# A weight quantisation is moved from inside phase 3 to the head of phase 4 of a two-layer kernel

## The chip, the cores and the metric

The kernel runs on all 8 cores of one Trainium2 chip, as one program on each core, with no exchange between the cores. The metric is the device time of one execution in microseconds (us), that of the slowest core.

## The reference, cut to what matters

Two transformer-like layers run in sequence on activations of 2 x 8192 tokens and 1024 features. What counts here is the last feed-forward block. Both of its weights are quantised to three levels before they are used:

```python
def weight_quant(w):
    scale = 1.0 / jnp.clip(jnp.mean(jnp.abs(w)), 1e-05)
    return jnp.clip(jnp.round(w * scale), -1, 1) / scale

def bit_linear(x, w):
    xq = x + jax.lax.stop_gradient(act_quant(x) - x)
    wq = w + jax.lax.stop_gradient(weight_quant(w) - w)
    return jnp.einsum('bsd,hd->bsh', xq, wq)

# L1_ffn: w1 is 4096 x 1024, w2 is 1024 x 4096, both float32
h = bit_linear(x, w1)
h = silu(depthwise_conv1d(h) )
y = bit_linear(h, w2)
# whole model, in order; each block is followed by x = layernorm(x + block(x))
# L0 attention, L0 feed-forward (quantised, low-rank), L1 attention, L1 feed-forward
```

The mean of the absolute values is taken over a whole weight, so a weight has to be read once for the mean and a second time to be rounded.

## The kernel before

Each core has its own share of the tokens as columns (`NCOL` = 2080, features on the partitions in `DCH` = 8 chunks of 128), and the program has four phases, one for each block of the model, with a wait of all engines between them (`_phase_gate`). The instruction stream of each engine is in the order in which the Python code emits it: nothing is reordered, so an instruction that waits holds up everything behind it on its engine. SP issues most DMAs, and its queue is in order too.

**Phase 3** (`emit_phase3`, layer 1 attention) first normalises, then runs two halves over the `WvT` weight and two over `WuT`. Each half loads 1024 weight columns into `w3w` by a DMA from GpSimd's queue and runs over `NT` = 5 tiles of `ST` = 416 columns: that is 20 tiles. In each tile `emit_xn` makes the normalised input (one small matmul, one ScalarE copy `a3sb`, eight GpSimd products `XB<-X,a3sb`), and then 8 output chunks of 8 matmuls each go to `p3psv`, ScalarE applies Silu into `p3u`, and VectorE writes `g_all`. After the 20 tiles GpSimd issues the load of `w3o` (`WoT`), 640 matmuls `p3psv<-g_all,w3o` follow, and a post-layernorm ends the phase.

**The quantisation of w1 and w2** is cut into steps by `wquant_steps` (line 1873) with units of 128 x 512: for each weight an `init`, 64 steps `p1` (load of 256 KB, VectorE sum of absolute values), one step `mid` (mean, its reciprocal, both spread over the partitions), 64 steps `p2` and a `fin`: 131 steps for a weight, 262 in all. A `p2` step is: SP loads the unit again (`wqs`), VectorE multiplies by the scale and adds a large constant (`wqc<-wqs`), GpSimd subtracts the constant (`wqc<-wqc,wqg`), which leaves the rounded value, VectorE clips to -1..1 (`wqc<-wqc`), VectorE multiplies by 1/scale into bfloat16 (`wqo<-wqc`), and SP stores the unit to device memory (`w1qd` or `w2qd`). SP waits for the last VectorE operation of a unit before it issues its store, and only then issues the next unit's load, so the second load buffer isn't used ahead of time in this pass. After each of the 20 tiles `drain_wq(k, 6)` emits six steps, 120 in all; when the tiles are done `drain_wq(k)` emits the other 142 in one piece, and all engines wait for the end of that before the load of `w3o`.

**Phase 4** (`emit_phase4`) starts when `X` has been spilled to device memory. It loads the two quantised weights, 8.4 MB each in bfloat16, and runs eight column blocks. It also has an `if not io.get("wquant_done")` branch (line 1329), which before isn't taken, with two calls of `emit_wquant` (line 1242). That function does the same arithmetic in the same order on the same engines, from SP's queue too, but with units that are a whole chunk: 8 units of 128 x 4096 for w1 (2 MB of float32 each), 32 of 128 x 1024 for w2 (512 KB each). Its second pass is, cut:

```python
for ch in range(nch):
    b = ch % 2
    vd = k.dma(q, wstr[b][:], src_h[:, ch, :], f"wq{q}e{b}")      # SP: load a unit
    v1 = k.tsc("vector", scr[:], wstr[b][:], swpp[:, 0:1], MAGIC, ALU.mult, ALU.add, inc="p4q1")
    k.wait("gpsimd", "p4q1", v1)
    v2 = k.tt("gpsimd", scri, scr[:], mgt[:].broadcast_to([128, width]), ALU.subtract, inc="p4q2")
    k.wait("vector", "p4q2", v2)
    v3 = k.tsc("vector", scri, scri, 1.0, -1.0, ALU.min, ALU.max, inc="p4q3")
    v4 = k.tsc("vector", wqo[b][:], scri, swpp[:, 1:2], None, ALU.mult, inc="p4q4")
    k.wait(q, "p4q4", v4)                                         # SP waits, then stores
    k.dma(q, wq_dram[:, ch * width:(ch + 1) * width], wqo[b][:], f"wq{q}o{b}")
```

Here too the load of the next unit stands behind the store of this one on SP's queue. In the first pass the load of unit `ch` waits for the reduction of unit `ch - 2`, so two loads can be under way.

Of the kernel before, what the change touches and what calls it, by code (L numbers as in the profile page):

```python
# [261 lines left out]
def alloc_common(k, io, stream=True):  # L262
    if stream:
        k.t["X"] = k.sb("X", [128, DCH * NCOL], F32)
        k.t["XB"] = k.sb("XB", [128, DCH * NCOL], BF16)
    k.t["ones1_f"] = k.sb("ones1f", [1, 128], F32)
    k.t["onescol_f"] = k.sb("onescolf", [128, 1], F32)
    k.t["onesn_bf"] = k.sb("onesnb", [128, 1], BF16)
    k.t["iden_f"] = k.sb("idenf", [128, 128], F32)
    k.t["iden_b"] = k.sb("idenb", [128, 128], BF16)  # L270
    k.t["eps_ln"] = k.sb("epsln", [128, 1], F32)
    k.t["neg1"] = k.sb("neg1", [128, 1], F32)
    k.t["ones1_b"] = k.sb("ones1b", [1, 128], BF16)
    k.dma("sync", k.t["ones1_f"][:], io["ones1"], "cst")
    k.dma("gpsimd", k.t["onesn_bf"][:], io["onesn"], "cstg")
    k.dma("gpsimd", k.t["ones1_b"][:], io["ones1"], "cstg")
    k.dma("sync", k.t["iden_f"][:], io["iden"], "cst")
    k.dma("gpsimd", k.t["iden_b"][:], io["iden"], "cstg")
    k.memset("vector", k.t["eps_ln"][:], 1e-5, inc="cstv")
    k.memset("vector", k.t["neg1"][:], -1.0, inc="cstv")  # L280
    k.memset("vector", k.t["onescol_f"][:], 1.0, inc="cstv")
    for eng in ("tensor", "vector", "scalar"):
        k.wait(eng, "cst", k.val("cst"))
        k.wait(eng, "cstg", k.val("cstg"))
        k.wait(eng, "cstv", k.val("cstv"))
# [11 lines left out]
def emit_load_stream(k, io):  # L297
    X, XB = k.t["X"], k.t["XB"]
    src = io["xin"].rearrange("(c p) n -> p c n", p=128)
    k.dma("sync", X[:].rearrange("p (c n) -> p c n", c=DCH), src, "ldx")  # L300
    k.dma("gpsimd", XB[:].rearrange("p (c n) -> p c n", c=DCH), src, "ldxb")
    for eng in ("tensor", "vector", "scalar", "gpsimd"):
        k.wait(eng, "ldx", k.val("ldx"))
        k.wait(eng, "ldxb", k.val("ldxb"))
# [402 lines left out]
def io_names(io):  # L707
    return {kk: ap.tensor.name for kk, ap in io.items() if hasattr(ap, "tensor")}
# [1092 lines left out]
def _phase_gate(k, sem, val):  # L1801
    for eng in K.ENGINES:
        k.wait(eng, sem, val)


def build_fused():
    stack = ExitStack()
    nc = bass.Bass("TRN2", target_bir_lowering=False)
    io = declare_io_fused(nc)
    with stack:  # L1810
        k = K(nc, stack)
        alloc_common(k, io, stream=False)
        k.push_scope()
        k.t["X"] = k.sb("X", [128, DCH * NCOL], F32)
        k.t["XB"] = k.sb("XB", [128, DCH * NCOL], BF16)
        emit_load_stream(k, io)
        s1, v1 = emit_phase1(k, io)
        _phase_gate(k, s1, v1)
        k.release_sems(("p1", "ldx"))
        k.dma("sync", io["xspill"], k.t["X"][:], "fsp1")  # L1820
        k.wait("sync", "fsp1", k.val("fsp1"))
        io["x1ref"] = io["xspill"]
        s2, v2 = emit_phase2(k, io)
        _phase_gate(k, s2, v2)
        k.release_sems(("p2", "dq_", "fsp1"))
        io["wquant_on"] = True
        io["wquant_done"] = True
        s3, v3 = emit_phase3(k, io)
        _phase_gate(k, s3, v3)
        k.release_sems(("p3", "wq_"))  # L1830
        k.dma("sync", io["xspill"], k.t["X"][:], "fsp2")
        k.wait("sync", "fsp2", k.val("fsp2"))
        _phase_gate(k, "fsp2", k.val("fsp2"))
        k.pop_scope()
        io["xstate"] = io["xspill"]
        s4, v4 = emit_phase4(k, io)
        k.wait("sync", s4, v4)
        k.finalize()
    return nc, io_names(io)
# [13 lines left out]


FUSED = True


def kernel_fused(**inputs):
    P = host_prep(inputs)
    Qs = [host_core_inputs(P, c) for c in range(NCORES)]  # L1860
    nc, nm = _built("fused", build_fused)
    maps = [{nm[kk]: v for kk, v in fused_in_map(P, Qs[c]).items()} for c in range(NCORES)]
    r = run_bass_kernel_spmd(nc, maps, core_ids=list(range(NCORES)))
    return host_assemble_yout([r.results[c][nm["yout"]] for c in range(NCORES)])
# [102 lines left out]
```

How the kernel before makes its waits and increments, by code:

```python
    def _post(self, eng, fn, inc, inck):  # L93
        if inc is None:
            self.ops[eng].append(fn)
            return None
        s = self._sem(inc)
        s[1] += inck
        h = s[0]
        self.ops[eng].append(lambda e, fn=fn, h=h, k=inck: fn(e).then_inc(h, k))
        return s[1]
# [1 line left out]
    def wait(self, eng, sem, v):  # L103
        if not v:
            return
        h = self._sem(sem)[0]
        assert v <= self._sem(sem)[1], f"wait beyond emitted incs: {sem} {v}"
        self.ops[eng].append(lambda e, h=h, v=v: e.wait_ge(h, v))
# [50 lines left out]
    def barrier(self, tag):  # L159
        s = self._sem("bar_" + tag)
        h = s[0]
        s[1] += len(self.ENGINES)
        tgt = s[1]
        for eng in self.ENGINES:
            self.ops[eng].append(lambda e, h=h: e.nop().then_inc(h, 1))
        for eng in self.ENGINES:
            self.ops[eng].append(lambda e, h=h, t=tgt: e.wait_ge(h, t))
```

## Time and profile before

| | us |
|---|---|
| median of 2 runs | 6435.69 |
| the 2 runs | 6421.44, 6449.95 |
| profiled execution | 6414.45 |
| its slowest core (core 2), first to last instruction | 6412.9 |
| the other cores | 6379.2 to 6409.1 |

Busy shares of the span on core 2: TensorE 35%, VectorE 31%, GpSimd 23%, ScalarE 13%; the DMA queues moved 258.92 MB. No engine is near full, so the time is a chain of waits between engines, and what a stage costs has to be read in that stage. The granted TensorE clock is given as a share of 2.4 GHz; 0.50 is its lower level, 1.2 GHz. Names in the rows are the program's buffers; "L136" is the line of the helper that records the operation. A unit of KB in a DMA row is 1024 bytes.

### The profile page before, as it was taken

Reading aid. Unit: us, or ns where it says so; the run is one execution under the profiler, and the core shown is the slowest. Engines: PE = TensorE matmul, PEld = TensorE weight load, DVE = VectorE, ACT = ScalarE, POOL = GpSimd, SP = SyncE. Lnnn points to the kernel's source line nnn. Section 1 sums busy time; section 2 is a strip of 40 time slices with the busy share of each in tenths; the row PEclk is TensorE's granted clock in tenths of the full one; section 3 lists DMA queues with packets and bytes.
Section 4 is the critical chain, followed back from the end, with each engine's and each line's share of the span. In section 5 each row is a group of like instructions: output and inputs, shape, how many; then the busy total and the mean of one; then the engine's idle time right before and its main releaser. Section 6 shows DMA issues by size and latency. Waiting matters only on the chain.

```text
span 6412.9 us, 40031 instructions; the slowest of 8 cores (6379.2 to 6412.9 us)
## 1 busy us (share of the span) xinstructions
PE 2256.0 (35%) x11801; PEld 1181.2 (18%) x11808; DVE 1972.1 (31%) x3257; ACT 856.2 (13%) x1551; POOL 1444.9 (23%) x1032
## 2 busy tenths in 40 slices
PE   1345423634636633532120000722424334323243
PEld 0111101211212211211010000411313223222132
DVE  0023432333333343432222222233333243333333
ACT  0000032322322223110000000020000000010000
POOL 0000030111101133322220111333243333332333
PEclk8665556766767765766565555855656556665566
DMA  9830033011030011221213221131000000000000
GB/s 150 112 46 1 0 85 85 1 54 52 1 92 7 1 54 25 73 59 40 53 39 103 73 59 55 27 112 53 14 0 14 14 0 14 1 13 14 0 14 7
DMA packets 167364, 258.92 MB, mean 40 GB/s; under 512 B 20681, under 2 KB 99666, under 8 KB 165330
## 3 DMA queue, kind: packets, MB, share of 16 engines
q1 hardware_dynamic: 116818, 202.25, 10.2%
q0 software_dynamic: 50336, 54.11, 6.2%
q8 instruction: 102, 1.67, 0.1%
q14 instruction: 108, 0.88, 0.1%
HBM read 268.22 MB, written 42.21 MB: 48 GB/s over the span
## 4 chain that ended last, share of the span: by engine, by line
PE 33%; DMA 19%; DVE 19%; POOL 14%; issue 8%; ACT 5%; SPq 1%; DVEq 1%; another core or an unknown queue 0%; POOLq 0%; ACTq 0%
PE p4pm L120 8%; PE psm L120 7%; PE p3psv L120 6%; DMA wqsw2T<-w2T 5%; POOL p4tB L136 5%; POOL p4tA L136 4%; DMA xkv<-xT 4%; POOL XB L136 3%; DMA wqsw1T<-w1T 3%; DVE p4tA L136 2%; DMA qbuf<-qTw 2%; DVE Y L136 2%; DVE X L136 2%; DVE p4cmt L148 2%; DMA p4x<-xspill 2%
## 5 line engine op out<-in xcount | busy, mean ns | idle before, releaser
L120 PE MATMUL p3psv<-XB,w3w 128*128 128x416 bf16 x1280 | 273.0, 382 | 432.9 <-POOL XB L136 432.7
L136 POOL TENSOR_TENSOR Y<-Y,p2asb 128x416 f32<-128x416 f32 x120 | 144.4, 1236 | 1211.3 <-ACT p2bsb L127 1211.3
L120 PE MATMUL p4pm<-p4xq,w1q 128*128 128x260 bf16 x2048 | 266.2, 297 | 399.2 <-DVE p4h L136 316.5
L136 POOL TENSOR_TENSOR p4tB<-p4h,cw 128x2048 f32<-128x2048 bf16 x64 | 296.9, 4640 | 414.1 <-DVE p4h L136 281.9
L120 PE MATMUL p4pm<-p4c,w2q 128*128 128x256 bf16 x2048 | 241.9, 284 | 229.9 <-DVE p4c L140 229.9
L120 PEld LDWEIGHTS p4pm<-p4xq,w1q 128*128 128x128 bf16 x2048 | 211.6, 105 | 457.5 <-issue 407.4
L120 PE MATMUL p3psv<-g_all,w3o 128*128 128x416 bf16 x640 | 115.4, 344 | 468.2 <-DMA w3o<-WoT 468.2
L120 PEld LDWEIGHTS p4pm<-p4c,w2q 128*128 128x128 bf16 x2048 | 207.8, 102 | 267.5 <-issue 235.5
L120 PEld LDWEIGHTS p3psv<-XB,w3w 128*128 128x128 bf16 x1280 | 136.6, 108 | 567.0 <-issue 490.7
L120 PE MATMUL psm<-VB,w2b 128*128 128x416 bf16 x960 | 213.9, 371 | 14.5 <-ACT t1s L127 14.5
L136 DVE TENSOR_TENSOR p4tA<-p4tA,p4tB 128x2048 f32<-128x2048 f32 x64 | 146.7, 2293 | 234.5 <-POOL p4tB L136 234.4
L136 POOL TENSOR_TENSOR XB<-X,a3sb 128x416 bf16<-128x416 f32 x160 | 167.2, 1077 | 219.1 <-ACT a3sb L127 219.1
L123 PE MATMUL p4pt<-idenb,p4c 128*128 128x128 bf16 x512 | 64.7, 306 | 417.0 <-ACT p4c L132 333.9
L120 PE MATMUL psm<-XB,w2b 128*128 128x416 bf16 x960 | 194.9, 347 | 14.2 <-ACT t1s L127 14.2
L136 POOL TENSOR_TENSOR p4tA<-p4c,p4rb 128x2048 f32<-128x2048 bf16 x32 | 130.5, 4077 | 300.7 <-ACT p4rb L127 232.9
L136 POOL TENSOR_TENSOR X<-X,asb_pl 128x416 f32<-128x416 f32 x120 | 154.7, 1321 | 187.4 <-ACT bsb_pl L127 187.4
L127 ACT CAST XB<-X 128x416 bf16<-128x416 f32 x162 | 82.8, 537 | 819.7 <-POOL X L136 645.1
L120 PE MATMUL pskv<-xkv,qkvT 128*128 128x512 bf16 x249 | 99.3, 565 | 246.4 <-DMA xkv<-xT 245.5
L136 POOL TENSOR_TENSOR wqcw2T<-wqcw2T,wqgw2T 128x512 f32<-128x512 f32 x64 | 66.5, 1038 | 497.6 <-DVE wqcw2T L140 497.6
L136 DVE TENSOR_TENSOR X<-X,bsb_pl 128x416 f32<-128x416 f32 x120 | 151.5, 1329 | 84.2 <-POOL X L136 84.1
L136 DVE TENSOR_TENSOR p4h<-p4pm,p4rb 128x260 bf16<-128x260 f32 x256 | 109.1, 429 | 189.8 <-PE p4pm L120 158.7
L136 POOL TENSOR_TENSOR wqcw1T<-wqcw1T,wqgw1T 128x512 f32<-128x512 f32 x64 | 66.5, 1038 | 444.9 <-DVE wqcw1T L140 444.9
(243 smaller groups left out, 4369.0 us busy)
## 6 DMA issues: line engine op xcount, KB each, us to landing
xkv<-xT POOLq DMA_DIRECT2D x32, 1024.0 KB, 16.1
wqsw1T<-w1T SPq DMA_DIRECT2D x128, 256.0 KB, 2.9
wqsw2T<-w2T SPq DMA_DIRECT2D x128, 256.0 KB, 3.0
qbuf<-qTw SPq DMA_DIRECT2D x96, 256.0 KB, 3.6
sbuf<-sTe SPq DMA_DIRECT2D x96, 256.0 KB, 4.1
xspill<-X SPq DMA_DIRECT2D x2, 8320.0 KB, 25.9
X<-xin SPq DMA_DIRECT2D x1, 8320.0 KB, 48.0
xrb<-xspill SPq DMA_DIRECT2D x5, 1664.0 KB, 9.2
```

What stands on the lines that cost most here:

```text
L120: e.matmul(o, l, r, start=s, stop=p), inc, 1)
L123: return self._post("tensor", lambda e, o=out, i=in_, d=iden: e.transpose(o, i, d), inc, 1)
L127: return self._post(eng, lambda e, o=out, i=in_: e.copy(o, i), inc, 1)
L136: e.tensor_tensor(o, a, b, p), inc, 1)
L148: e.tensor_reduce(o, i, AXX, p, apply_absolute_value=a), inc, 1)
```

## The change

Phase 3 is built with `wquant_on` unset, and phase 4 with `wquant_done` unset.

```diff
@@ build_fused
         k.release_sems(("p2", "dq_", "fsp1"))
-        io["wquant_on"] = True
-        io["wquant_done"] = True
+        if WQ_IN_P3:
+            io["wquant_on"] = True
+            io["wquant_done"] = True
         s3, v3 = emit_phase3(k, io)
@@
 FUSED = True
+WQ_IN_P3 = False
```

So `wquant_steps` is never called, the `drain_wq` calls in phase 3 find no steps and emit nothing, and the fence after phase 3's statistics is for GpSimd alone. In phase 4 the two calls of `emit_wquant` are now emitted, ahead of the loads of the quantised weights: w1 with 8 units of 4096 columns, then w2 with 32 units of 1024 columns.

## Rows read from the trace of the kernel before

**Rows 1.** The page, the span in 40 slices of 160 us: TensorE's busy tenths.
```profile
PE   1345423634636633532120000722424334323243
```

**Rows 2.** Chain that ended last, 2400 to 4500 us: start us, us, what.
```profile
2524.37 8.18 POOL XB L136 x8
2547.86 8.33 POOL XB L136 x8
...
2659.93 8.18 POOL XB L136 x8
...
2780.07 17.88 DMA w3w<-WuT
2799.56 8.18 POOL XB L136 x8
...
2950.41 8.56 POOL XB L136 x8
...
3008.17 8.55 POOL XB L136 x8
...
4007.06 25.55 DMA w3o<-WoT
```

**Rows 3.** Instructions on w1's load buffer: duration min/median/max ns, first to last start.
```profile
L140 DVE TENSOR_SCALAR wqcw1T<-wqsw1T,wqww1T x64: 479/486/489, 2858.6 to 3437.4; 128x512 f32<-128x512 f32 x64
```

**Rows 4.** The same of w2's load buffer, scratch and output buffer.
```profile
L148 DVE TENSOR_REDUCE wqpw2T<-wqsw2T x64: 678/686/687, 3445.6 to 3561.0; 128x1 f32<-128x512 f32 x64
L140 DVE TENSOR_SCALAR wqcw2T<-wqsw2T,wqww2T x64: 486/486/489, 3568.2 to 4001.5; 128x512 f32<-128x512 f32 x64
...
L136 POOL TENSOR_TENSOR wqcw2T<-wqcw2T,wqgw2T x64: 1038/1038/1040, 3568.8 to 4002.2; 128x512 f32<-128x512 f32 x64
L140 DVE TENSOR_SCALAR wqcw2T<-wqcw2T x64: 426/427/428, 3570.0 to 4003.3; 128x512 f32<-128x512 f32 x64
L140 DVE TENSOR_SCALAR wqow2T<-wqcw2T,wqww2T x64: 485/486/489, 3570.5 to 4003.9; 128x512 bf16<-128x512 f32 x64
```

**Rows 5.** Timeline 3552 to 3580 us, w2's first rounding step: start us, us, instruction.
```profile
3568.19 0.49 DVE L140 TENSOR_SCALAR wqcw2T<-wqsw2T,wqww2T 128x512 f32<-128x512 f32 x1 [4.49 <-DMA wqsw2T<-w2T]
...
3571.08 0.33 SPq L116 DMA_DIRECT2D w2qd<-wqow2T  x1
3571.45 0.43 SPq L116 DMA_DIRECT2D wqsw2T<-w2T  x1
3575.14 0.49 DVE L140 TENSOR_SCALAR wqcw2T<-wqsw2T,wqww2T 128x512 f32<-128x512 f32 x1 [4.14 <-DMA wqsw2T<-w2T]
```

**Rows 6.** Granted clock by stretch: from:to, us, PE busy, PEclk, DMA share, GB/s.
```profile
4008.00:4034.00 26.00, 0.94 (x3) 0.50 0.91 162
4034.00:4045.00 11.00, 11.00 (x51) 0.79 0.00 0
```

**Rows 7.** Groups with shapes, phase 4 (4360 us on): busy, mean ns of one, idle before.
```profile
L136 POOL TENSOR_TENSOR p4tA<-p4c,p4rb 128x2048 f32<-128x2048 bf16 x32 | 130.5, 4077 | 300.7 <-ACT p4rb L127 232.9 <-DVE p4c L140 67.8
L136 POOL TENSOR_TENSOR p4tA<-p4tA,cb 128x2048 f32<-128x2048 f32 x32 | 115.2, 3601 | 81.3 <-DVE p4tA L136 81.3
L148 DVE TENSOR_REDUCE p4cmt<-p4pt 128x1 f32<-128x1024 bf16 x78 | 95.6, 1225 | 142.2 <-PE p4pt L123 142.2
L140 DVE TENSOR_SCALAR p4tA<-p4tA 128x2048 f32<-128x2048 f32 x32 | 39.3, 1227 | 180.9 <-POOL p4tA L136 180.9
```

**Rows 8.** DMA issues of the whole span: count, KB each, median us from issue to landing.
```profile
wqsw1T<-w1T SPq DMA_DIRECT2D x128, 256.0 KB, 2.9
wqsw2T<-w2T SPq DMA_DIRECT2D x128, 256.0 KB, 3.0
...
xspill<-X SPq DMA_DIRECT2D x2, 8320.0 KB, 25.9
...
xrb<-xspill SPq DMA_DIRECT2D x5, 1664.0 KB, 9.2
p4x<-xspill SPq DMA_DIRECT2D x8, 1040.0 KB, 8.3
w1qd<-wqow1T SPq DMA_DIRECT2D x64, 128.0 KB, 1.7
...
w2q<-w2qd SPq DMA_DIRECT2D x1, 49.4
```

## The prediction

> **What bounds the kernel now.** I read the page's slices first. TensorE is nearly empty from slice 22 to 25 and thin from 18 on [rows 1]; that is the stretch of phase 3 in which the quantisation runs. The chain that ended last then tells what fills it. In the first half of phase 3 a tile begins with eight GpSimd products and the next begins 23.5 us later (2524.37 to 2547.86), and a half of five tiles with its weight load takes 135.6 us (2524.37 to 2659.93) and 139.6 us (2659.93 to 2799.56) [rows 2]. In those halves the six steps behind each tile are of kind `p1`, and the first tile, with none before it, is as long as the others, so `p1` costs nothing there: its loads and sums lie beside the next tile's GpSimd products and matmuls. From the mean on it is another picture: the tile of 2950.41 is followed by that of 3008.17, 57.8 us later [rows 2]. Six `p2` steps stand in VectorE's, GpSimd's and SP's order between two tiles, and TensorE's next tile needs GpSimd's products. They hide almost nothing: 57.8 - 23.5 = 34.3 us for six steps, 5.7 each, against 6.9 where they run alone ((4001.5 - 3568.2) / 63) [rows 4]. The last 10 `p2` steps of w1 and all of w2 then run with no tile beside them: w1's last begins at 3437.4 [rows 3], and the load of `w3o` is issued at 4007.06 [rows 2]. So about 570 us of the path is the bare drain, and some 380 more are the steps put between tiles. A step itself is latency: a load of 256 KB that lands after 3.0 us [rows 8], and four operations that wait for each other.
>
> **The change, part by part.**
>
> *Removed from phase 3.* Without steps the 20 tiles should run like the first two halves. The mean of a half with its load is (135.6 + 139.6) / 2 = 137.6 us; the load's share is 2799.56 - 2780.07 = 19.5 us. From 2524.37 the four halves end after 3 x 137.6 + (137.6 - 19) = 531 us, at 3056 us. There GpSimd issues the load of `w3o`, which now is at 4007.1 [rows 2]. The gain is 951 us. The u halves have one VectorE operation for each output chunk where the v halves have two, so nothing there makes them longer. Bounds for the tile: 23.5 to 24 us, that is 5 us either way on the sum.
>
> *Not changed.* The matmuls on `w3o` begin with a clock of 0.50 after a wait for that load and rise in the first 11 us [rows 6]; after the change they come after the same 26 us wait. Phase 4's blocks begin after a stretch without matmuls in both kernels. I count nothing for the clock. The fences that fall away in phase 3 cost nothing, since the tile behind them waits for the weight load anyway. The spill of `X` and the loads of the quantised weights are as before.
>
> *Added at the head of phase 4.* Nothing runs beside it, so each microsecond counts. I need the operations at 4096 and 1024 columns, which the trace doesn't have, and scale each from two widths.
>
> - VectorE scaling and clipping: 427 ns at 512 columns [rows 4] and 1227 at 2048 [rows 7], so 0.521 ns a column more: 0.69 us at 1024, 2.29 at 4096. The two with a scale from memory are 0.06 longer (486) [rows 4]: 0.75 and 2.35. Bounds: in proportion from 486 at 512 (3.9 at 4096), and twice the 2048 row (2.45).
> - GpSimd's subtraction: 1038 ns at 512 with a broadcast second input [rows 4], 3601 at 2048 with a broadcast one, 4077 with one full row of 256 repeated [rows 7]. The operand here is a broadcast, so I go by 3601: 1.67 ns a column, 1.89 us at 1024 and 7.02 at 4096. Upper bound: eight times 1038, 8.3 us. No row gives a lower price.
> - VectorE's sum: 686 ns at 512 [rows 4], 1225 at 1024 [rows 7]: 1.05 a column, 4.45 us at 4096.
> - Loads: 256 KB land after 2.9 to 3.0 us. The big contiguous transfers are the spill, 8320 KB in 25.9 us (329 GB/s with its start), and the two quantised weights, 16.8 MB in 49.4 us (340 GB/s), with all eight cores about at the same place [rows 8]. At 340 GB/s each further MB takes 2.9 us: 3.7 us for 512 KB, 2.9 + 1.84 MB / 340 GB/s = 8.3 for 2 MB. Bounds: the 1664 KB load at 185 GB/s and the 1040 KB load at 128 GB/s [rows 8], both with short rows (1664 and 1040 bytes), where these have 16 and 4 KB; so I go by 340.
>
> First pass of w1: eight loads, two under way, in effect a stream of 16.8 MB, 49 us at 340 GB/s, and 2 us of start and the last sum of 4.5: 56. First pass of w2: at 512 columns one unit takes (3561.0 - 3445.6) / 63 = 1.83 us, which is (load 2.98 + sum 0.69) / 2 [rows 4]. At 1024 it is (3.75 + 1.23) / 2 = 2.5, 32 units 80, with the start 83.
>
> Second pass. A step of 512 columns has period 3575.14 - 3568.19 = 6.95 us: 2.80 from the first VectorE operation to the end of the last (2.44 of work, 0.36 between), 0.46 until the next load is issued behind the store, and 3.69 until that has landed [rows 5]. For w2: 0.75 + 1.89 + 0.69 + 0.75 + 0.36 = 4.45; 0.46; and 3.69 + 0.77 for the larger load + 0.38 for the larger store ahead of it = 4.84. Period 9.75, times 32 = 312 us. For w1: 2.35 + 7.02 + 2.29 + 2.35 + 0.36 = 14.4; 0.46; and 3.69 + 5.4 for 1.84 MB more of load + 2.7 for 0.92 MB more of store = 11.8. Period 26.6, seven of them and a first of 8.5 + 14.4: 209 us.
>
> The two means: the last sum ends at 3561.0 + 0.7 [rows 4] and the first rounding operation begins at 3568.2 [rows 5], 6.5 us, of which 3.0 are the first load, counted already: 3.5 each, 7 for two. The last stores have to land: 128 KB take 1.7 us [rows 8], so 1.7 + 2.7 = 4.4 for w1's 1 MB, and 1.7 + 0.4 for w2's, with the issue 2.7.
>
> Gates and memsets I put at 1.5 (estimated from the 0.46 between waits). Sum: 56 + 209 + 83 + 312 + 7 + 4.4 + 2.7 + 1.5 = 676 us. Fewer and larger units help: 64 rounding steps of 6.9 us are 440 in w2 and 32 of 9.75 are 312; for w1 eight of 26.6 are 209.
>
> *Two prices from the Trainium skill, by themselves.* Its page GPSIMD Engine Reference, section Performance versus the Vector engine, gives 4497 ns for a two-input GpSimd operation at 2048 float32 columns; the trace has 3601 and 4077 for a broadcast second input, which is lower, so I go by the trace. By the page the subtraction would be an estimated 9.0 us at 4096 and 2.3 at 1024, and the sum 676 + 8 x 2.0 + 32 x 0.4 = about 705 us. Its page DMA: Bandwidth & Descriptors, section Anatomy of one DMA, fits 2.0 us plus the bytes at 436 GB/s for one transfer, an estimated 6.8 us for 2 MB where I have 8.3, and by it the sum would be some 45 us smaller, first passes included; the trace has 340 GB/s for its longest transfers, so I keep that.
>
> **Net.** -951 + 676 = -275 us. The sum is made on the profiled execution: 6414 - 275 = 6139 us. The median of the two runs is 21 us above that execution, and 6436 - 275 = 6161. I forecast between the two: 6150 us, 4.4% less than the median.
>
> **The rivals.**
>
> - *Loads are slow at this size when eight cores read at once.* The added work moves 67.1 MB of loads and 16.8 of stores, 83.9 MB, of which I priced nearly all at 340 GB/s, 247 us. For it: 2 MB units make the DMA engines busier than anything in phase 3 now. Against it: the 49.4 us of the two weights. At the 185 GB/s of the 1664 KB load it is 454 us, 207 more: 6150 + 207 = 6357 us, 1.2% less than before, so no change that can be told.
> - *The same with the rate of the 1040 KB load, 128 GB/s:* 655 us, 408 more, 6558 us, slower by 1.9%. It has eaten the gain of 286 us from 157 GB/s down (83.9 MB / 533 us), and slower by over 2% begins at 127. Only short rows have shown such a rate.
> - *The interleaved steps were in fact covered,* and the long tiles are long for another reason (GpSimd's products wait for something else). Then phase 3 gives back only the bare drain, 4007 - 3437 = 570 us, and the time is 6150 + 381 = 6531 us, 1.5% slower. What speaks for it is that something must overlap; the Trainium skill's page Trainium Kernel Development and Optimization, section Best Practices, asks for double-buffering so that DMA and compute overlap, and moving the work to a stage of its own gives that up. Against it: 57.8 us a tile with six rounding steps, 23.5 with six sums or none [rows 2], and the next load stands behind the store on SP's queue, so there is no overlap within a step now either. By the page's rule the trace disagrees for `p2` and agrees for `p1`.
> - *Transfers start sooner than I have it.* The 128 KB stores land in 1.7 us, which is 1.3 besides the bytes where I have 2.1 for a load: 0.8 less on 40 rounding loads and half of it on 40 in the first passes, 48 us less, 6102. It is a variant of the forecast, in its range.
>
> **How the numbers follow.** The forecast with that variant has 0.90, loads at the middle rate 0.05, at the low rate 0.02, covered steps 0.03. A measurement of this kernel tells about 2% (129 us) from no change. Faster by over 2% is below 6307 us: all of the first case but little, 0.91. Within 2%: most of the rest, 0.07. Slower by over 2%: 0.02. For the range I take the bounds of the unknown prices: below, the variant at 6102, less 11 for the lower base, 5 for the tiles and 26 for what else may be cheaper: 6060. Above, GpSimd in proportion (16 more in all), VectorE in proportion (8 x 4.2 and 32 x 0.6, 53) and all bytes at 300 GB/s, a quarter of the way to 185 (33): 102 more, 6250. About 0.85 of the chance is in it.
>
> **What would show each step.** Tiles of phase 3 all 23 to 24 us apart, and `w3o` issued near 3056. In phase 4: eight GpSimd subtractions of about 7.0 us, 32 of 1.9; load landings near 11 and 4 us (8 and 4 in the first pass); a w2 rounding period near 9.75 and a w1 one near 26.6; 676 us from the end of the spill to the load of `w1q`. The forecast is wrong if the tiles stay long without steps, if the landing of 2 MB is over 15 us, or if phase 4's blocks take another time than now.

## The result, and the profile after

| | before | after |
|---|---|---|
| median of all runs, us | 6448.3 (10 runs) | 6102.2 (11 runs) |
| ratio, with its 95% interval | | 0.9468 (0.9436 to 0.9500) |
| profiled execution, us | 6414.5 | 6166.7 |

The forecast was 6150 us with a range of 6060 to 6250. In a second comparison on another occasion the ratio was 0.9521 (0.9476 to 0.9565), so the gain is 308 to 343 us, where the sum had 275.

The page of the changed kernel, its slices (154 us each), again shows four empty slices of TensorE, but one phase later: they lie between phase 3's layernorm and phase 4's blocks. What is gone are the thin slices ahead of them, 18 to 21 in [rows 1].

```profile
PE   1345431663662663355575000012432424324243
DMA  9840015003003001000010534240000000000000
```

In the profiled execution, 65 us above the median, cores 0 to 3 show a granted clock of 0.62 and spans about 40 us longer than cores 4 to 7 at 0.635, so phase 3 is read on core 5 (the chain that ended last: start us, us, what), the head of phase 4 on core 1, the slowest.

```profile
2526.26 8.18 POOL XB L136 x8
2550.25 8.32 POOL XB L136 x8
...
2795.68 8.18 POOL XB L136 x8
2819.78 8.19 POOL XB L136 x8
...
3001.16 8.49 POOL XB L136 x8
3025.08 8.19 POOL XB L136 x8
3049.72 27.16 DMA w3o<-WoT
```

The tiles are 23 to 24 us apart in the last half as in the first, where they were 57.8 [rows 2], and the load of `w3o` is issued 523 us after the first tile. Then the head of phase 4, the first units of w1 and the last of w2:

```profile
3406.22 24.31 DMA xspill<-X
3431.03 15.03 DMA wqsw1T<-w1T
...
3496.50 7.74 DMA wqsw1T<-w1T
3504.33 2.36 DVE wqcw1T L140
3506.83 7.02 POOL wqiw1T L136
3513.95 2.31 DVE wqiw1T L140
3516.35 2.37 DVE wqow1T L140
3519.15 9.19 DMA wqsw1T<-w1T
3528.51 2.36 DVE wqcw1T L140
...
4059.95 2.03 DMA w2qd<-wqow2T
4065.28 49.70 DMA p4x<-xspill
```

A w1 unit takes 24.2 us (3504.33 to 3528.51), of which 9.2 are the landing of its load; the first load, with no store ahead of it, lands after 7.7. The same for w2 on core 1, from the instructions on its load and scratch buffers and a piece of the timeline:

```profile
L148 DVE TENSOR_REDUCE wqpw2T<-wqsw2T x32: 1219/1220/1221, 3697.2 to 3773.8; 128x1 f32<-128x1024 f32 x32
L140 DVE TENSOR_SCALAR wqcw2T<-wqsw2T,wqww2T x32: 753/753/755, 3781.7 to 4055.3; 128x1024 f32<-128x1024 f32 x32
L136 POOL TENSOR_TENSOR wqiw2T<-wqcw2T,wqgw2T x32: 1892/1892/1892, 3782.6 to 4056.3; 128x1024 f32<-128x1024 f32 x32
```

```profile
3794.99 0.33 SPq L116 DMA_DIRECT2D w2qd<-wqow2T  x1
3795.40 0.38 SPq L116 DMA_DIRECT2D wqsw2T<-w2T  x1
3799.12 0.75 DVE L140 TENSOR_SCALAR wqcw2T<-wqsw2T,wqww2T 128x1024 f32<-128x1024 f32 x1 [4.21 <-DMA wqsw2T<-w2T]
3800.08 1.89 POOL L136 TENSOR_TENSOR wqiw2T<-wqcw2T,wqgw2T 128x1024 f32<-128x1024 f32 x1 [6.82 <-DVE wqcw2T L140]
3802.08 0.69 DVE L140 TENSOR_SCALAR wqiw2T<-wqiw2T 128x1024 f32<-128x1024 f32 x1 [2.20 <-POOL wqiw2T L136]
3802.95 0.75 DVE L140 TENSOR_SCALAR wqow2T<-wqiw2T,wqww2T 128x1024 bf16<-128x1024 f32 x1 [0.18 <-DVE wqiw2T L140]
```

The period is (4055.3 - 3781.7) / 31 = 8.83 us. The load was issued right behind the store at 3795.40 and used at 3799.12, 3.7 us later. The step of [rows 5] had 3.69 us for 256 KB, but on core 2. On core 1 of both kernels these loads land after 2.9 us (256 KB) and 3.5 us (512 KB) at the median, so the larger load does take longer.

All kernels side by side, in stages that the same four instructions bound on each core: the first tile of phase 3, the issue of `w3o`'s load, the issue of the spill behind phase 3, the issue of `w1q`'s load. Each number is the median over the eight cores of one profiled execution, in us. The lines "before" and "changed" are of the first comparison, "changed, again" to "sums in phase 3" of a second, "before, again" and the last three of a third.

| kernel | to the first tile | tiles and steps | `w3o`, layernorm | spill and head of phase 4 | rest |
|---|---|---|---|---|---|
| before | 2521 | 1463 | 267 | 25 | 2114 |
| before, again | 2546 | 1470 | 267 | 25 | 2115 |
| changed | 2561 | 531 | 280 | 660 | 2104 |
| changed, again | 2532 | 530 | 266 | 663 | 2104 |
| steps after the tiles | 2525 | 1601 | 269 | 25 | 2113 |
| w1 in units of 1024 | 2534 | 521 | 269 | 773 | 2111 |
| sums in phase 3 | 2529 | 543 | 267 | 506 | 2109 |
| next load ahead | 2530 | 520 | 266 | 459 | 2105 |
| ... and rounding on VectorE | 2532 | 521 | 268 | 364 | 2108 |
| all three | 2537 | 546 | 268 | 210 | 2111 |

So 936 us leave the stage of the tiles and 637 come in at the head of phase 4.

### The profile page after: what moved, and what is told of

It is laid out like the page before. It is cut to its first block, busy times and chain, and to the rows that moved or that the text cites. A ratio compares the mean times of both kernels' runs of the same rounds, so it can differ in the third digit from the quotient of the medians.

```text
span 6165.1 us, 38230 instructions; the slowest of 8 cores (6101.2 to 6165.1 us)
## 1 busy us (share of the span) xinstructions
PE 2357.5 (38%) x11808; PEld 1200.6 (19%) x11808; DVE 1902.6 (31%) x2905; ACT 857.7 (14%) x1551; POOL 1424.6 (23%) x944
## 4 chain that ended last, share of the span: by engine, by line
PE 36%; DVE 19%; DMA 17%; POOL 15%; issue 7%; ACT 5%; SPq 1%; DVEq 0%; ACTq 0%; POOLq 0%; another core or an unknown queue 0%
PE psm L120 8%; PE p4pm L120 8%; PE p3psv L120 7%; POOL p4tB L136 5%; DMA xkv<-xT 4%; POOL p4tA L136 4%; DMA wqsw2T<-w2T 3%; POOL XB L136 3%; DVE p4tA L136 3%; DMA qbuf<-qTw 2%; DVE Y L136 2%; DMA wqsw1T<-w1T 2%; DVE X L136 2%; DMA p4x<-xspill 2%; DVE p4cmt L148 2%
## 5 line engine op out<-in xcount | busy, mean ns | idle before, releaser
L120 PE MATMUL p3psv<-XB,w3w 128*128 128x416 bf16 x1280 | 308.5, 418 | 191.1 <-POOL XB L136 190.3
L120 PE MATMUL psm<-VB,w2b 128*128 128x416 bf16 x960 | 233.4, 396 | 14.5 <-ACT t1s L127 14.5
L120 PE MATMUL psm<-XB,w2b 128*128 128x416 bf16 x960 | 216.3, 375 | 14.2 <-ACT t1s L127 14.2
L123 PE MATMUL p4pt<-idenb,p4xq 128*128 128x128 bf16 (+1 forms) x192 | 24.3, 305 | 496.6 <-DVE p4xq L128 454.2
L144 DVE SCALAR_TENSOR_TENSOR X<-psm,biasA,X 128x416 f32<-128x416 f32 x120 | 78.1, 651 | 269.6 <-PE psm L120 269.6
L136 DVE TENSOR_TENSOR Y<-Y,p2bsb 128x416 f32<-128x416 f32 x120 | 120.5, 1004 | 126.2 <-POOL Y L136 126.2
L148 DVE TENSOR_REDUCE p4cmt<-p4pt 128x1 f32<-128x1024 bf16 (+1 forms) x88 | 107.7, 1224 | 154.8 <-PE p4pt L123 154.8
```

Source lines behind the costliest of these rows:

```text
L120: e.matmul(o, l, r, start=s, stop=p), inc, 1)
L123: return self._post("tensor", lambda e, o=out, i=in_, d=iden: e.transpose(o, i, d), inc, 1)
L136: e.tensor_tensor(o, a, b, p), inc, 1)
L144: e.scalar_tensor_tensor(o, a, s, b, p0, p1), inc, 1)
L148: e.tensor_reduce(o, i, AXX, p, apply_absolute_value=a), inc, 1)
```

## The experiments

### The steps moved behind the tiles, nothing else

The kernel before with both `drain_wq(k, 6)` calls taken out:

```diff
                       ALU.mult, ALU.add, inc=f"p3mx{oc % 2}")
-            drain_wq(k, 6)
@@
                 k.tt("vector", gch, gch, uch, ALU.mult, inc=f"p3mx{oc % 2}")
-            drain_wq(k, 6)
```

> The kernel before with the two drain calls behind the 20 tiles taken out: all 262 steps of 512 columns run in one piece behind the tiles, nothing else changes. My theory (a rounding step is a chain that covers nothing, a sum step between tiles is free): the tiles are 23.5 to 24 us apart throughout, as in the first halves; the piece takes 2 x (64 x 1.83 + 6.5 + 64 x 6.9 + 2) = about 1135 us where it was 566; the load of w3o comes at 3056 + 1135 = about 4190 us, 185 us later than before, ratio to before about 1.029. Rival (the long tiles had another reason, the steps in them were covered): the tiles of the u halves stay near 58 us, and the time is about 565 us longer, ratio 1.09. Rival (it was the interleaving itself that cost, and the size of a unit doesn't matter): the piece takes no more than the 630 us that the same work takes at the head of phase 4, ratio about 0.95.

Measured: 1.0251 (1.0210 to 1.0291), which is 161 us (135 to 187). The tiles are 22.5 to 24.2 us apart in all four halves; these are some of the last half (chain that ended last), and the roundings of w1 behind them (scratch buffer of w1):

```profile
2940.40 8.18 POOL XB L136 x8
2963.47 8.19 POOL XB L136 x8
```

```profile
L140 DVE TENSOR_SCALAR wqcw1T<-wqsw1T,wqww1T x64: 485/486/489, 3184.1 to 3596.8; 128x512 f32<-128x512 f32 x64
```

The rival that the long tiles had another reason falls. The rival that the size of a unit doesn't matter falls too: the bare piece takes 1080 us (1601 less the 521 of tiles alone) for the work that the changed kernel does in 637. And it says where the gain of the change does not come from: with the same units, taking the steps out from between the tiles is a loss, 1601 - 1466 = 135 us. The interleaving had been worth something. Of the 120 steps between the tiles 64 are sums, which take 64 x 1.83 = 117 us by themselves (an estimate), and 54 are rounding steps, 5.7 us each between tiles and 6.5 alone. From this comes off what the sums cost the weight loads (below); the 135 us were not split further. I had 185 for it; the piece was 1135 in my sum and 1080 on the chip, since a rounding step takes (3596.8 - 3184.1) / 63 = 6.55 us here, not 6.9.

### The changed kernel again

> The changed kernel once more, unaltered. In its profiled execution the cores 0 to 3 showed a lower clock (0.62) and matmul stretches of 15 to 16 us a tile where cores 4 to 7 had 14 to 14.5 us. Theory: that is of the execution, not of the change; this profile has all cores near 0.64 and a phase 3 from the first tile to the load of w3o of about 524 us on the slowest core, as core 5 had. Rival: the denser matmuls of phase 3 lower the clock on the slowest core each time; then that stretch is again about 550 us.

Measured: 0.9521 (0.9476 to 0.9565). All eight cores are at 0.633 to 0.638, and the stage of the tiles takes 518 to 533 us, where it was 552 on cores 0 and 1 of the first profile. Cores 0 and 1 have 518 and 519 us now, so their long stage belongs to that execution. The groups of the two cores of it, core 1 and then core 5, show the price (busy us, mean ns of one matmul | idle before):

```profile
L120 PE MATMUL p3psv<-XB,w3w 128*128 128x416 bf16 x1280 | 308.5, 418 | 191.1 <-POOL XB L136 190.3 <-ACT p3u L132 0.8
```

```profile
L120 PE MATMUL p3psv<-XB,w3w 128*128 128x416 bf16 x1280 | 279.4, 389 | 190.9 <-POOL XB L136 190.9
```

The idle time is the same, the 29 us are in the matmuls. But the rival holds in part. On six cores of the repeat, 2 to 7, some tiles are 25 to 26 us apart as well; from 2500 to 3080 us the granted clock is 0.70 on core 7 and 0.75 on core 1. In the two kernels that have the rounding steps in phase 3, no tile without such steps is more than 24.2 us behind the one before it in its half. Nor is one in the run with the next load ahead, so the spells come and go also with the tiles of the changed kernel; what starts them is open. They are worth about 10 us of the stage: 530 us against the 520 of undisturbed cores.

### w1 in four times as many units

```diff
-        emit_wquant(k, io, "w1T", io["w1qd"], DCH, DH)
+        emit_wquant(k, io, "w1T", io["w1qd"], DCH, DH, upc=4)   # 32 units of 1024 columns
```

> The changed kernel with w1 quantised in 32 units of 1024 columns in place of 8 of 4096, w2 as it is. My theory (the price of a unit is its fixed part, load latency and waits, plus columns): w1's sums take about 80 us in place of 62, its roundings 32 x 8.8 = 282 in place of 8 x 24.3 = 194, together about 106 us more than the changed kernel, ratio to before about 0.963. Rival (bytes and columns set the cost, the size of a unit does not): no difference to the changed kernel, 0.947.

Measured: 0.9719 (0.9678 to 0.9761), 0.0198 above the changed kernel in the same comparison, which is 127 us; the head of phase 4 takes 773 us, 110 more than 663. The sums and roundings of w1 (instructions on its load buffer):

```profile
L148 DVE TENSOR_REDUCE wqpw1T<-wqsw1T x32: 1219/1220/1222, 3392.3 to 3472.9; 128x1 f32<-128x1024 f32 x32
L140 DVE TENSOR_SCALAR wqcw1T<-wqsw1T,wqww1T x32: 752/753/755, 3482.0 to 3760.6; 128x1024 f32<-128x1024 f32 x32
```

82 us of sums and 32 x 8.99 = 288 of roundings, where 80 and 282 were expected. The price of a unit is a fixed part and its columns: a rounding unit took 6.55 us at 512, 8.8 to 9.0 at 1024 and 24.3 at 4096, so about 4.0 us and 5.0 us for each 1024 columns, and only the fixed part can be saved by a larger unit.

### The first pass back in phase 3

The steps keep `p1` and `mid` alone (seven behind each tile), their result `swpp` lives outside the phases, and `emit_wquant` loses its first pass:

```diff
-            drain_wq(k, 6)
+            drain_wq(k, 7)          # both places; steps are 64 sums and the mean, per weight
@@ emit_wquant
-    swpp = k.sb(f"wqw{which}", [128, 2], F32)
-    for ch in range(nch): ...      # loads, sums, mean
+    swpp = k.t["swpp" + which]
```

> The changed kernel with the first pass (sums and means) of both weights put back between the tiles of phase 3 in units of 512 columns, seven steps behind each tile, and only the rounding pass at the head of phase 4. My theory (sum steps between tiles are covered): tiles stay 23.5 to 24 us apart, phase 4's head is shorter by 62 + 82 = 144 us, ratio to before 0.947 - 0.022 = 0.925. Rival (the steps cost in a tile about what they cost alone, 1.8 us each, since VectorE and SP are held): phase 3 is longer by up to 128 x 1.8 = 230 us and the ratio is 0.947 or above.

Measured: 0.9297 (0.9261 to 0.9333), 0.0224 under the changed kernel in the same comparison, 144 us. By stages the head is 157 us shorter and the stage of the tiles 13 longer than in the repeat, 22 longer than in the kernels at 520 or 521. All tiles but the last keep their distance; two other things get longer. One is the weight load between two halves (chain that ended last of this kernel, core 3, then the landings of `w3w`'s loads on core 5 of the changed one, min/median/max us):

```profile
2722.07 8.32 POOL XB L136 x8
...
2745.80 8.32 POOL XB L136 x8
...
2798.13 18.00 DMA w3w<-WuT
...
2937.37 19.14 DMA w3w<-WuT
```

```profile
DMA to landing us min/median/max: 12.9/13.1/13.4
```

The other is the last tile, on the same chain:

```profile
3028.93 8.20 POOL XB L136 x8
...
3053.52 2.60 DMA wqtw2T<-w2T
...
3059.03 0.98 PE wqps L120 x4
3060.01 0.38 PE p3psa L120
...
3061.23 0.24 POOL XB L136
```

So a sum step costs nothing in a tile, but one behind the last tile of a half loads beside the weight that the next half waits for: the three loads inside the stage take 15.3 to 20.7 us over the eight cores, 17.3 at the median, 4 us more each. And the step with w2's mean stands in TensorE's order ahead of the last tile's first matmul and waits for the last sums: that tile comes 32.3 us behind the one before (32.1 to 32.6 on all cores) and not 23.9. Three loads and this one tile make the 22 us.

### The next load ahead of the store

```diff
+    vds = [k.dma(q, wstr[c][:], src_h[:, c, :], f"wq{q}e{c}") for c in range(2)]
     for ch in range(nch):
-        if ch >= 2:
-            k.wait(q, "p4q1", k.val("p4q1") - 1)
-        vd = k.dma(q, wstr[b][:], src_h[:, ch, :], f"wq{q}e{b}")
         ...
+        if ch + 2 < nch:                       # behind the first operation of unit ch
+            k.wait(q, "p4q1", v1)
+            vds.append(k.dma(q, wstr[b][:], src_h[:, ch + 2, :], f"wq{q}e{b}"))
```

> The changed kernel with one order altered in the rounding pass: SP issues the load of unit ch + 2 as soon as unit ch has been read, ahead of the store of unit ch, so the next unit's load no longer stands behind this unit's store. My theory (in a rounding period the load's landing and the arithmetic are added, 9.2 + 14.6 us in w1 and 3.5 + 4.5 in w2): the landing goes out of the chain, periods fall from 24.3 to about 14.5 and from 8.8 to about 4.6 us, in all about 200 us less than the changed kernel, ratio to before about 0.95 - 0.031 = 0.919. Rival (the memory is what limits, with eight cores loading at once): w2's period stays above 6 us and the gain is under 100 us, ratio above 0.935.

Measured: 0.9197 (0.9137 to 0.9257); the head of phase 4 takes 459 us, 204 less (by the two ratios 0.0324, about 208 us). Timeline of two w2 units:

```profile
3644.59 1.89 POOL L136 TENSOR_TENSOR wqiw2T<-wqcw2T,wqgw2T 128x1024 f32<-128x1024 f32 x1 [2.53 <-DVE wqcw2T L140]
...
3649.01 1.89 POOL L136 TENSOR_TENSOR wqiw2T<-wqcw2T,wqgw2T 128x1024 f32<-128x1024 f32 x1 [2.52 <-DVE wqcw2T L140]
```

The period is 4.4 us here and 4.5 over all 32, the arithmetic alone; w1's is 14.4. The landing was in the chain, and the memory keeps up with eight cores at this pace.

### Rounding on VectorE alone

GpSimd's subtraction is folded into the two VectorE operations behind it:

```diff
-        v2 = k.tt("gpsimd", scri, scr[:], mgt[:].broadcast_to([128, width]), ALU.subtract, inc="p4q2")
-        v3 = k.tsc("vector", scri, scri, 1.0, -1.0, ALU.min, ALU.max, inc="p4q3")
-        v4 = k.tsc("vector", wqo[b][:], scri, swpp[:, 1:2], None, ALU.mult, inc="p4q4")
+        v3 = k.tsc("vector", scri, scr[:], MAGIC, 1.0, ALU.subtract, ALU.min, inc="p4q3")
+        v4 = k.tsc("vector", wqo[b][:], scri, -1.0, swpp[:, 1:2], ALU.max, ALU.mult, inc="p4q4")
```

> As the run with the next load ahead, and the four operations of a rounding made three, all on VectorE (scale and add the constant; subtract it and cap at 1; bound at -1 and multiply by 1/scale), so GpSimd and its wait are out of the chain. My theory: a w1 unit takes 3 x 2.35 + 0.2 = 7.3 us if its 2 MB load and 1 MB store keep up (3.1 MB at 340 GB/s are 9.3 us, so rather 9.3), a w2 unit about 2.4 us, another 40 + 70 = 110 us less, ratio about 0.902. Rival (GpSimd's part was already covered by something): within 20 us of the run before it, 0.919.

Measured: 0.9058 (0.9008 to 0.9109), head 364 us, 95 less than the run before it, 110 expected. First operations of a unit on core 4, w1 and w2 (load buffers), two of w1's on the timeline, and the stretch of w1's rounding and that of w2's (from:to, us, ... DVE busy ..., PEclk, DMA share, GB/s):

```profile
L140 DVE TENSOR_SCALAR wqcw1T<-wqsw1T,wqww1T x8: 2347/2353/2354, 3492.8 to 3552.7; 128x4096 f32<-128x4096 f32 x8
```

```profile
L140 DVE TENSOR_SCALAR wqcw2T<-wqsw2T,wqww2T x32: 746/753/755, 3653.6 to 3750.3; 128x1024 f32<-128x1024 f32 x32
```

```profile
3507.06 2.35 DVE L140 TENSOR_SCALAR wqcw1T<-wqsw1T,wqww1T 128x4096 f32<-128x4096 f32 x1
...
3517.13 2.35 DVE L140 TENSOR_SCALAR wqcw1T<-wqsw1T,wqww1T 128x4096 f32<-128x4096 f32 x1 [2.80 <-DMA wqsw1T<-w1T]
```

```profile
3492.80:3552.70 59.90, 0.00 (x0) 0.00 (x0) 48.83 (x21) 0.00 (x0) 0.00 (x0) 0.50 0.99 338
3655.00:3750.00 95.00, 0.00 (x0) 0.00 (x0) 65.84 (x92) 0.00 (x0) 0.00 (x0) 0.50 0.79 248
```

The w1 units are 8.6 us apart on the mean of this core, and 8.4 to 9.3 over the eight, but not evenly. The first three begin 7.1 us apart, which is VectorE's own time, as their loads had landed by then; the two after them come after 10 and 11 us, each behind its load. In these 60 us the DMA share is 0.99 at 338 GB/s, so here the transfers are the limit, as expected. A w2 unit takes 3.12 us and not 2.4: only two loads are under way, each lands after 4.5 to 5.8 us (5.3 at the median) and the next is issued when a buffer has been read. That was the step missing from my expectation.

### All three

> The three together: sums and means between the tiles of phase 3, next load ahead, rounding on VectorE alone. My theory: the gains add, as each takes a different part of the path: 0.902 less the 144 us (0.022) of the sums = 0.880, about 5660 us. Rival (with the sums in phase 3 and the faster pass in phase 4 some other wait takes over, such as TensorE's lower clock): 0.895 or above.

Measured: 0.8832 (0.8793 to 0.8872), a median of 5688.9 us against 6437.8 for the kernel before in the same comparison. It beats both kernels: about 7% under the changed one, whose ratios of 0.9468 and 0.9521 are of other comparisons. The head of phase 4 is 210 us, the stage of the tiles 546. The gains add but for the 25 us that the sums put on the stage of the tiles, on the weight loads and the last tile as above.

### The kernel before again

> The kernel before once more, unaltered, for a second trace. The profiled execution that the forecast was made on lies 21 us under the median of the first two runs and 34 under the median of ten. Theory: the spread comes from the landing times of the small loads in the rounding steps and in phase 1; this profile has rounding periods of 6.8 to 7.1 us in the bare piece and the load of w3o issued 1450 to 1490 us after the first tile.

Measured: cores 2 and 3 have rounding periods of 6.93 and 6.98 us, the other six 6.47 to 6.61, so the expectation fell for six cores; the stage of the tiles takes 1462 to 1501 us, as expected but for its upper end. Its median core is 45 us longer than in the first profile (6434 against 6389), and 25 of these come ahead of the first tile, 7 in the stage of the tiles. So the spread between executions isn't mainly one of the rounding steps. That the slowest core of the first profile, core 2, had 6.88 while most cores had 6.46 to 6.65 I had not looked at when I took its rows.

## Why the prediction was right

It forecast a gain of 275 us, and by stages the two pairs of profiles give 936 - 637 + 10 = about 310. The second comparison has 308 us, the first 343. The mechanism is as forecast. That the net came as near as it did is in part luck: the removed part was 15 us too large and the added part 39. Point by point:

*What is removed, 951 us.* The stage of the tiles is 1466 us before and 530 after, 936; on undisturbed cores it goes down to 520. The errors in the term offset each other. I took the drain from core 2, whose rounding steps are among the slowest: its stage before is 1483 us, 17 above the 1466. And I took a half of the tiles with its weight load from the halves that had sum steps beside them, one of whose `w3w` loads took 17.9 us to land [rows 2]; alone they land after 13. That made the 531 us 11 too long, and the spells of lower clock, for which I had nothing, put about 10 back.

*What is added, 676 us: 637 measured.* The operations came out within 1%: GpSimd 7012 ns at 4096 columns and 1892 at 1024, VectorE 2353, 2294 and 4420, as scaled from two widths [rows 4, 7]. The first passes took 62 us (56 in the sum) and 82 (83). The mis-sized term is the landing in the rounding pass. I put the store's bytes ahead of the load's at 340 GB/s: 11.8 us for w1, 4.84 for w2 with issue and wake. Measured were 9.4 (9.2 of landing) and 3.7, which is 8 x 2.4 and 32 x 1.1 = 54 us of the sum. On core 1 w1's rounding took 193 us where the sum had 209, w2's 282 where it had 312. Two things are in this term. One is the core: the 3.69 us that it starts from are of core 2 and of a step of 6.95 us, and on core 1 of the kernel before a step takes (3970.3 - 3562.4) / 63 = 6.47 us:

```profile
L140 DVE TENSOR_SCALAR wqcw2T<-wqsw2T,wqww2T x64: 485/486/489, 3562.4 to 3970.3; 128x512 f32<-128x512 f32 x64
```

That is some 0.5 us of each unit. The other is the store. Alone a 2 MB load landed after 7.7 us, with a 1 MB store issued 0.4 us ahead after 9.2: the store cost 1.4 us, where its bytes at 340 GB/s would be 3.1.

*Costed at nothing.* The `w3o` matmuls and the layernorm stay at 266 to 269 us where the clock is as before. The rest of phase 4 is 10 us shorter, which I had not forecast. The matmuls there are a little quicker in the page's groups (core 2 before, core 1 after), 5.5 and 3.1 us less of busy time:

```profile
L120 PE MATMUL p4pm<-p4xq,w1q 128*128 128x260 bf16 x2048 | 266.2, 297 | 399.2 <-DVE p4h L136 316.5
...
L120 PE MATMUL p4pm<-p4c,w2q 128*128 128x256 bf16 x2048 | 241.9, 284 | 229.9 <-DVE p4c L140 229.9
```

```profile
L120 PE MATMUL p4pm<-p4xq,w1q 128*128 128x260 bf16 x2048 | 260.7, 293 | 398.9 <-DVE p4h L136 316.1
...
L120 PE MATMUL p4pm<-p4c,w2q 128*128 128x256 bf16 x2048 | 238.8, 282 | 229.5 <-DVE p4c L140 229.5
```

Why is open. The stage takes 2113 to 2115 us in the three profiles with the rounding steps in phase 3 and 2104 to 2111 in the seven with them in phase 4.

*The rivals.* Slow loads at 185 or 128 GB/s: excluded by the landings, and the run with the next load ahead has 459 us for the whole head. Covered steps: excluded for the tiles' length by the first experiment, but the argument behind it was not empty. The interleaving did cover 135 us, by the estimate above most of it in the sum steps; the prediction used this only as "costs nothing there" and its sum contains it (the removed 951 are what is left after covering). The rule of the Trainium skill (Trainium Kernel Development and Optimization, Best Practices, double-buffering so that DMA and compute overlap) turns out right in another place than the kernel before had it: the overlap was worth 204 us inside the rounding pass, once the next load no longer stood behind the store.

*The two page prices.* By the Trainium skill's page GPSIMD Engine Reference, section Performance versus the Vector engine, GpSimd's operation at 4096 columns was an estimated 9.0 us; it took 7.01 with a broadcast second input, so the trace disagrees there. By the Trainium skill's page DMA: Bandwidth & Descriptors, section Anatomy of one DMA, the 2 MB load was an estimated 6.8 us; alone it landed after 7.7, between the page's value and my 8.3.

## What to carry to other kernels

A pass that is made of small dependent steps is priced by its fixed part: the period of one step (landing, waits, issues) times their number, which two rows give, and it hides in other work only if no engine that the other work needs waits in it. So look first at what stands between a step's store and the next step's load on the issuing queue, then at the size of the step, and only then at where the pass lies. And when a stretch is taken from the trace as "undisturbed", check that nothing else was loading beside it, and that the core it is read on is like the others.

## What was not expected of the hardware

- Loads and stores under way together moved as much as loads alone: 338 GB/s at a DMA share of 0.99 over w1's rounding in the run on VectorE alone (core 4), with eight cores at it, against 340 GB/s for the 16.8 MB of the two weights. Yet the store ahead of a 2 MB load cost 1.4 us and not 3.1. The two directions were not tried apart.
- Loads of 256 KB on SP's queue beside a 2 MB weight load of GpSimd's queue lengthen that one from 13 us to 15 to 21.
- In both profiles of the kernel before, cores 2 and 3 took 6.9 to 7.0 us for a rounding step of w2 and the others 6.5 to 6.7; with the same steps run behind the tiles, cores 2 and 3 took 6.45 and 6.49. The cause is open.
- Tiles of the same matmuls came 23 to 24 us apart or, for a spell, 25 to 26, at a granted clock of 0.75 or 0.70 over the stage, on some cores and not on others of one execution.
